# Last weights copied to bf16 beside the convolution passes, router in single steps, and three smaller moves, in a fused convolution, attention and router kernel on eight cores

## The reference

```
xn = layernorm(x)
y  = conv1d(xn, conv_w, 3 taps, 'SAME') + conv_b       # 4096 -> 3 x 1024
q, k, v = split(y, 3)                                  # blocks of 128 tokens
qh, kh, vh = q@wq + bq, k@wk + bk, v@wv + bv           # 16 heads of 64
p  = softmax(causal(qh kh^T / 8))                      # inside each block
s  = (p vh) @ wo + bo;  s = s @ proj_w + proj_b        # 1024 -> 1024 -> 4096
r  = softmax(xn @ router_w^T + router_b)               # 64 experts
w  = r where it is among the 8 largest of its token, else 0
g  = silu(xn * sum(w) + w @ expert_bias)
out = x + s * g
```

## Time and profile before

| | us |
|---|---|
| median of 3 runs (range) | 1099.91 (1096.72 to 1100.67) |
| the profiled execution, its time | 1098.76 |
| its span, slowest core (core 1) | 1097.2 |
| spans of all cores | 1080.7 to 1097.2 |
| PE busy | 1014.8 (92%) |
| DVE busy | 719.1 (66%) |
| ACT busy | 448.0 (41%) |
| POOL busy | 164.6 (15%) |

### The profile page before, as it was taken

How to read it: one execution, slowest core, us unless ns; L and a number is a source line. 1 busy time by engine, 2 the same in 40 slices (tenths; PEclk the granted TensorE clock), 3 DMA queues, 4 the chain that set the end, 5 groups by cost and what they waited for, 6 DMA issues and landing times.

```text
span 1097.2 us, 16289 instructions; the slowest of 8 cores (1080.7 to 1097.2 us)
## 1 busy us (share of the span) xinstructions
PE 1014.8 (92%) x5196; PEld 467.1 (43%) x5196; DVE 719.1 (66%) x1102; ACT 448.0 (41%) x700; POOL 164.6 (15%) x191
## 2 busy tenths in 40 slices
PE   1468998999999999999999999999999999879997
PEld 1235543444444444444444444444444444323332
DVE  6898769666666256666666367777777554355565
ACT  4748533333333243333333255555555213534322
POOL 0134310000000000000000000001110133045555
PEclk9999999999999999999999999999999999989999
DMA  8942327667676587666666566767787798999883
GB/s 260 344 147 87 100 103 231 220 218 228 229 230 215 169 280 263 230 231 230 230 226 214 173 209 218 226 241 231 251 276 216 245 322 264 292 306 309 270 272 144
DMA packets 59072, 251.02 MB, mean 229 GB/s; under 512 B 7494, under 2 KB 7782, under 8 KB 56678
## 3 DMA queue, kind: packets, MB, share of 16 engines
q1 hardware_dynamic: 55372, 241.29, 67.5%
q0 software_dynamic: 2560, 8.57, 2.5%
q10 hardware_dynamic: 1056, 0.11, 0.1%
HBM read 227.05 MB, written 23.09 MB: 228 GB/s over the span
## 4 chain that ended last, share of the span: by engine, by line
PE 71%; DMA 13%; DVE 8%; issue 3%; ACT 2%; SPq 1%; POOL 1%; DVEq 0%; ACTq 0%; POOLq 0%
PE PS L218 69%; DVE AL L225 6%; DMA AL<-cw 4%; DMA AL<-x 4%; DMA AL<-pw 3%; ACT AL L229 2%; PE PS L222 2%; DMA AL<-wo 2%; DVE AL L265 1%; SPq L72 1%; DMA AL<-wv 0%; DMA AL<-eb 0%; ACT PS L231 0%; POOL AL L790 0%; DVEq L58 0%
## 5 line engine op out<-in xcount | busy, mean ns | idle before, releaser
L218 PE MATMUL PS<-AL 128*128 128x512 bf16 (+2 forms) x4608 | 948.0, 373 | 14.4 <-DVE AL L225 13.8
L218 PEld LDWEIGHTS PS<-AL 128*128 128x128 bf16 (+2 forms) x4608 | 418.0, 101 | 528.4 <-issue 62.7
L225 DVE TENSOR_TENSOR AL<-AL 128x512 bf16<-128x512 f32 (+1 forms) x578 | 386.3, 696 | 173.3 <-PE PS L218 118.6
L229 ACT ACTIVATE AL<-AL 128x1024 bf16<-128x1024 f32 (+1 forms) x221 | 232.7, 1055 | 374.7 <-PE PS L218 305.5
L225 DVE TENSOR_TENSOR AL<-PS,AL 128x512 bf16<-128x512 f32 (+2 forms) x145 | 115.5, 797 | 33.3 <-ACT AL L229 18.1
L225 POOL TENSOR_TENSOR AL<-AL 128x512 bf16<-128x512 f32 (+1 forms) x63 | 106.4, 1689 | 182.2 <-DVE AL L225 101.6
L222 PE MATMUL PS<-tI128f,AL 128*128 128x128 f32 (+2 forms) x300 | 44.9, 286 | 52.6 <-ACT AL L229 30.2
L960 DVE SCALAR_TENSOR_TENSOR AL<-AL,tSc,PS 128x1024 f32<-128x1024 f32 x32 | 41.0, 1280 | 65.0 <-PE PS L218 52.1
L229 ACT ACTIVATE AL<-PS 128x512 f32<-128x512 f32 (+2 forms) x88 | 56.8, 669 | 64.5 <-PE PS L222 36.7
L229 ACT ACTIVATE AL<-AL,tScb 128x1024 f32<-128x1024 f32 x32 | 36.8, 1151 | 86.1 <-DVE AL L960 86.1
L72 POOL DMA_DIRECT2D AL<-qhs x16 | 12.1, 756 | 346.6 <-PE PS L218 331.3
(11 more groups left out here) (52 smaller groups left out, 213.9 us busy)
## 6 DMA issues: line engine op xcount, KB each, us to landing
AL<-cw SPq DMA_DIRECT2D x192, 768.0 KB, 5.2
AL<-x SPq DMA_DIRECT2D x16, 1024.0 KB, 30.3
AL<-pw SPq DMA_DIRECT2D x32, 512.0 KB, 6.0
AL<-x SPq DMA_DIRECT2D x32, 512.0 KB, 9.4
out<-AL SPq DMA_DIRECT2D x31, 512.0 KB, 6.9
AL<-wq SPq DMA_DIRECT2D x8, 512.0 KB, 3.8
AL<-wk SPq DMA_DIRECT2D x8, 512.0 KB, 3.9
pts<-AL POOLq DMA_DIRECT2D x16, 256.0 KB, 5.9
```

Source lines behind the costliest of these rows:

```text
L218: return PE.do(lambda e: e.matmul(out, lhsT, rhs, start=start, stop=stop, skip_group_check=skip), *toks, tok=tok)
L225: return eng.do(lambda e: e.tensor_tensor(out, a, b, op), *toks, tok=tok)
L229: return AC.do(lambda e: e.activation(out, in_, func, bias=bias, scale=scale), *toks, tok=tok)
```

## The change

1. **Copies.** 24 new stream entries "copy", two in each of 12 passes (`COPY_P`; behind units 3 and 6). An entry loads one f32 block of `wo` (8), of the first (8) or of the second block of `proj_w` (8) into a staging slot, GpSimd casts it into one of two bf16 buffers that attention uses later (`pbf`, `pts`), and GpSimd's queue stores it to a new DRAM buffer `wbs`. The first attention block waits for the last two stores.
2. **End of the passes.** `wo` and blocks 0 and 1 are loaded from `wbs` in bf16, without staging or cast. Block 2 is staged and cast on GpSimd, block 3 staged and cast on ACT, both ahead of the output stage; `load3` and `cast3` are gone.
3. **x pieces** of the output stage are loaded on GpSimd's queue.
4. **Router.** The eight subtractions of the maximum become one operation with a broadcast operand; the eight masked steps one comparison into a mask `stm`; the eight scalings two products. `drip` gives an entry at units 1 to 4 of a pass only.
5. **v3** is formed by GpSimd while statistics are left (steps 0 to 10), and the even bank is then free when ACT has copied it.
6. **Slots** of attention blocks 7, 8 and 10 to 15 come one slot earlier.

```diff
+        COPY_P = (2, 4, 5, 6, 7, 9, 10, 11, 12, 13, 14, 15)
...
+                if p in COPY_P and g in (3, 6):
+                    stream.append(("copy", 0, 2 * COPY_P.index(p) + g // 6))
...
+            elif kind == "copy":
+                rows = slice(128 * (g % 8), 128 * (g % 8) + 128)
+                src = d_wo[rows, :] if g < 8 else d_pw[rows, 1024 * (g // 8 - 1):1024 * (g // 8)]
+                k = SY.dma(S(f"sF{f}"), fq[f], src, *f_free[f])
+                k = GP.do(lambda e: e.tensor_copy((pbf, pts)[g % 2], fq[f]), k, k_copy[g % 2], tok=True)
+                f_free[f] = [k]
+                k_copy[g % 2] = GP.dma(S(f"sWC{g % 2}"), d_wb[g], (pbf, pts)[g % 2], k)
...
-                k_v3 = tt(DV, vout(3), cc2(bE), E1, ALU.subtract, k_ec, k_p)
+                if n_stat < 32:
+                    tt(GP, vout(3), E0, E1, ALU.subtract, k_ec, k_p, tok=False)
+                    ring[rn % 3] = [k_ec]
+                else:
+                    ring[rn % 3] = [tt(DV, vout(3), cc2(bE), E1, ALU.subtract, k_ec, k_p)]
...
         def r_sub():
-            rd["k"] = each(lambda e, j: e.tensor_scalar(lgt3[:, j, :], lgt3[:, j, :],
-                                                        nm8[:, j:j + 1], None, ALU.add), 8, rd["k"])
+            rd["k"] = tt(DV, lgt3, lgt3, bc(nm8), ALU.add, rd["k"])
...
-            rd["k"] = each(lambda e, j: e.scalar_tensor_tensor(
-                lgt3[:, j, :], lgt3[:, j, :], t8a[:, 8 * j + 7:8 * j + 8], lgt3[:, j, :],
-                ALU.is_ge, ALU.mult), 8)
+            rd["m"] = tt(DV, stm, lgt3, bc(t8a3[:, :, 7]), ALU.is_ge)
 
         def r_norm():
-            rd["k"] = each(lambda e, j: e.tensor_scalar(lgt3[:, j, :], lgt3[:, j, :],
-                                                        rs8[:, j:j + 1], None, ALU.mult), 8, rd["k"])
+            k = tt(DV, lgt3, lgt3, bc(rs8), ALU.mult, rd["m"])
+            rd["k"] = tt(DV, lgt3, lgt3, stm, ALU.mult, k)
...
-        s_at = [1 + 33 * n // 10 for n in range(NHB)]
+        s_at = [1, 4, 7, 10, 14, 17, 20, 23, 26, 30, 33, 36, 39, 42, 46, 49]
...
-                dripped(1)
+                if 1 <= g <= 4:
+                    dripped(1)
...
         for kc in range(8):
-            k_wo = staged(GP, wob[kc], d_wo[128 * kc:128 * kc + 128, :], k_unit23[1])
+            k_wo = SY.dma(S("sWO"), wob[kc], d_wb[kc], *k_copy, k_unit23[1])
+        for i in range(2):
+            for kc in range(8):
+                k_pwl[i] = SY.dma(S(f"sPW{i}"), pwb[i][kc], d_wb[8 * (i + 1) + kc], k_unit23[7])
...
-            k_pwl[1] = stage_pw(AC, 1, kc, k_unit23[7])
+            k_pwl[2] = stage_pw(GP, 2, kc, k_unit23[7])
         for kc in range(8):
-            k_pwl[2] = stage_pw(AC, 2, kc)
+            k_pwl[3] = stage_pw(AC, 3, kc, k_vpe)
...
-                x_tok[m] = SY.dma(S(f"sXG{m % NX}"), xg[m % NX],
+                x_tok[m] = GP.dma(S(f"sXG{m % NX}"), xg[m % NX],
                                   two(d_x[t][:, 1024 * i:1024 * i + 1024]), w)
```

More of the change, by code:

```diff
@@ L111, in build_program @@
     d_pt = dint("pts", [16, 128, 1024])
+    d_wb = dint("wbs", [24, 128, 1024])
     d_pbs = nc.dram_tensor("pbs", [2, 32, 128], BF16, kind="Internal").ap()
@@ L173, in build_program @@
         t8a = f32v(B_KH + 6144, 64)
+        stm = f32v(B_KH + 8192, 512).rearrange("p (j f) -> p j f", j=8)
         nm8 = f32v(B_KH + 6400, 8)
@@ L340, in build_program @@
                 slot += 1
+                if p in COPY_P and g in (3, 6):
+                    stream.append(("copy", 0, 2 * COPY_P.index(p) + g // 6))
         for kind, _, _ in stream:
             ui.append(nu % NU)
-            nu += kind != "w"
+            nu += kind not in ("w", "copy")
         f_free = [[k_ed] for _ in range(NF)]
@@ L347, in build_program @@
         u_ready = [None] * len(stream)
+        k_copy = [None, None]
         def prep(n):
@@ L474, in build_program @@
                     osb[e][:, :, 0:1], edge[:, a:a + 2, s:s + 1]), tok=True)
-                k_v3 = tt(DV, vout(3), cc2(bE), E1, ALU.subtract, k_ec, k_p)
+                if n_stat < 32:
[3 more added lines that the diff above has]
+                    ring[rn % 3] = [tt(DV, vout(3), cc2(bE), E1, ALU.subtract, k_ec, k_p)]
                 k_v0 = tt(GP, vout(0), O0, O1, ALU.subtract, k_ec, k_oc, k_p)
-                tt(DV, vout(1), E0, cc2(bO), ALU.add, k_oc, tok=False)
+                tt(DV, vout(1), E0, cc2(bO), ALU.add, k_ec, k_oc, tok=False)
                 k_v2 = tt(DV, vout(2), cc2(bO), E0, ALU.subtract)
-                ring[rn % 3] = [k_v3]
                 ring[(rn + 1) % 3] = [k_v2]
@@ L553, in router_pe1, with bc @@
             return rd["k"]
+        def bc(z):
+            return z.unsqueeze(2).to_broadcast([128, 8, 64])
         def r_max():
@@ L699, in at_nrm @@
             k = DV.do(lambda e: e.reciprocal(t_rr[:, o:o + 8], t_rs[:, o:o + 8]), a[n]["exp"], tok=True)
-            if n >= 1:
-                DV.wait(a[n - 1]["t"])
+            DV.wait(a[n - 1]["t"] if n >= 1 else k_copy[0])
             a[n]["nrm"] = tt(DV, pbf.rearrange("p (q t) -> p q t", q=8),
@@ L714, in at_pts @@
         def at_pts(n):
-            if n >= 1:
-                AC.wait(a[n - 1]["sp"])
+            AC.wait(a[n - 1]["sp"] if n >= 1 else k_copy[1])
             a[n]["pts"] = act(pts, bT, AF.Copy, a[n]["t"])
@@ L763, in build_program @@
                     evac(p)
-            elif kind != "w":
+            elif kind in ("q", "k"):
                 if g == 0:
@@ L795, in stage_pw @@
             return staged(eng, pwb[i][kc], d_pw[128 * kc:128 * kc + 128, 1024 * i:1024 * i + 1024], *toks)
-        for kc in range(8):
-            k_wo = staged(GP, wob[kc], d_wo[128 * kc:128 * kc + 128, :], k_unit23[1])
-        k_z = DV.do(lambda e: e.memset(pbhl, 0.0), k_unit23[7], tok=True)
         k_pwl = [None] * 4
         for kc in range(8):
-            k_pwl[0] = stage_pw(GP, 0, kc, k_unit23[7])
+            k_wo = SY.dma(S("sWO"), wob[kc], d_wb[kc], *k_copy, k_unit23[1])
+        k_z = DV.do(lambda e: e.memset(pbhl, 0.0), k_unit23[7], tok=True)
+        for i in range(2):
+            for kc in range(8):
+                k_pwl[i] = SY.dma(S(f"sPW{i}"), pwb[i][kc], d_wb[8 * (i + 1) + kc], k_unit23[7])
         for i in range(2):
@@ L924, in build_program @@
         w_last = []
-        k_st3 = [None] * 8
-        def load3(k):
-            if k < 8:
-                k_st3[k] = SY.dma(S(f"sST{k % 4}"), stg[k % 4],
-                                  d_pw[128 * k:128 * k + 128, 3072:4096], *st_free[k % 4])
-        def cast3(k):
-            k_pwl[3] = act(pwb[3][k], stg[k % 4], AF.Copy, k_st3[k], k_vpe)
-            st_free[k % 4] = [k_pwl[3]]
         for m in range(NX):
             load(m)
-            if m < 4:
-                load3(m)
         PE.wait(last["o"], a[7]["o"], *vfree[0], *vfree[1], k_eb, k_pb)
@@ L965, in build_program @@
                 finish(m - 1)
-            if m in range(2, 18, 2):
-                cast3(m // 2 - 1)
-                load3(m // 2 + 3)
         finish(NM - 1)
```

## The result

The changed kernel takes 1118.8 us (median; 1116.0 to 1120.6, and one execution of 1168.0) against 1099.9 us for the kernel before: a ratio of 1.0175, 95% interval 1.0144 to 1.0206. In the execution of 1168.0 the cores of one die had a granted clock of 0.92 to 0.95 where the others had 0.99; executions of that kind are left out of all medians, ranges and ratios here. The kernel is slower by 19 us where 14 us less were forecast. The profiled execution took 1119.94 us. Here, as there, the slowest core counts, and now all eight are late.

The account below looks back on a forecast made before the run. TensorE's work plus a few holes was taken as the bound, with DVE the bound from 40 to 84 us. Terms -6.5 - 4.3 + 1.5 - 4.4 = -13.7 gave 1085.1, median 1086 us; range 1077 to 1096.

Parts of the forecast that it names:

- Copies, "I take +1.5 us": Copies beside the 12 passes: mostly hidden, costing 1.5 us in all.
- rival 3: Copies starve the passes: slots turn in 9.06 us, passes 30.2 us, total 1116, starting above 6.8 us latency; chance 0.06 in full.
- mean 7.3: hidden: Copy passes: conv loads hold slots 7.6 us, copies about 6; mean 7.3 fits the 8.3 us available per turn.
- the latency at 5.5 us: Copy passes: assumed conv load latency, giving 7.6 us in a slot with about 2.1 us of transform.
- the cast at 1.04 us: Copy passes: each copy's GpSimd cast takes 1.04 us, on an engine said to be idle there.
- the rule for two SBUF inputs: GpSimd and a two-SBUF-input DVE operation exclude each other for a whole instruction; early differences were judged to lose nothing.
- The share of 0.88: Passes with two copies: DMA share rises from 0.67 to about 0.88.
- Early differences, -6.5 us: Transposing stage, steps 0 to 10: DVE, the bound, gives GpSimd one of three differences, saving 11 x 0.593 = 6.5 us.
- rival 4: Transposing stage: GpSimd or ACT paces the early steps, shrinking the 6.5 us gain to 1 or 2; total 1091, chance 0.06.
- Router, -4.3 us: Start of pass 2: the 3.05 us hole shrinks, gaining 2.65 us, plus 1.7 us of clock; together 4.3 us.
- Slots, taken as 0 with bounds ±2: Attention: moved slots shift which evacuations have an exp block ahead; holes of 0.3 to 1.6 us merely change place.
- End, -4.4 us: Before output piece 2: the first Silu waits behind ACT's fourth-block casts instead of late x; TensorE resumes 4.4 us earlier.

Follow-up runs that it names:

- no_copies: Changed kernel with last weights and output stage as before, keeping early differences, router and slots: 1089.7 us, ratio 0.9893.
- own_place: Changed kernel with copy loads in a buffer of their own, each still taking an unused turn in the staging rotation: 1119.5 us, ratio 1.0185.
- own_slot: Changed kernel with copy loads in a buffer of their own, taking no place in the staging rotation: 1090.8 us, ratio 0.990.
- router_only: Kernel before with only the router's steps of the change: 1100.1 us, ratio 1.0009.

## Why the prediction was wrong

- **Copies, "I take +1.5 us": the step that failed.** The passes lost 28 us against before and 30 against no_copies, which is rival 3 in full where 1.5 were forecast: 12 passes of 30.1 us (27.6 + 30.0/12) where that rival has 30.2. Rival 3 says 1116 us in all, and 1118.8 were measured. Three things in the step were wrong.
  - It averaged the turns ("mean 7.3: hidden"), as if a copy that is done in 6 us gave its spare time to the unit loads. It cannot: loads are issued in order, and the slot passed over is the next unit's loss; own_place gives a copy no time in a slot at all and is as slow, where the average would be 0.8 x (6.0 + 2.1) = 6.5 us a turn of the 8.3 at hand. (With 6.8 us of latency the step has 8.5 for the mean turn and rival 3 has 8.3; the terms give 8.3.)
  - It took the latency at 5.5 us as something given, when the places themselves bunch the loads, to 9.01 us in the chain above.
  - It took the cast at 1.04 us and at no cost to DVE, though it had the rule for two SBUF inputs in hand and tried it on the early differences: the transforms' sums have two such inputs, and in the changed kernel the casts lengthened 18 of them per core. How the 30 us divide between late loads and lengthened sums is open.
- **Rival 3 had it.** With a turn of 3/10 of 30.1, that is 9.0 us, a latency of 5.9 and 2.1 of transform leave 1 us of waiting for the list ahead; the 9.06 us between issues in the earlier trace rows already held all of it. The row that measured the turn directly was in hand and was given a chance of 0.06, because the sum from parts came out lower. That it hits the pass to 0.1 us is in part luck, since it was taken beside other traffic: two empty places give 28.1 us a pass, a turn of 8.4. That its start was put at 6.8 us of latency was wrong too: own_slot runs at 6.6 without a loss, and the changed kernel starves at 5.9.
- **The share of 0.88 was reachable.** own_slot has 0.91 with no hole, so "GpSimd is idle there" and the DMA engines' room were rightly judged. The order of the slots was not, nor what the casts do to DVE's sums.
- **Early differences, -6.5 us: right.** End of pass 0 is at 149.7 us on the mean core against 155.2, so 5.5 us; rival 4 is out. No run has these differences alone; nothing else of the change stands ahead of that point.
- **Router, -4.3 us: mis-sized.** It was read on core 1, where pass 2 went from 32.5 to 27.6 us, as forecast (4.9). But the mean core won 1.5 us in the passes (2.8 in pass 2, less 1.3 in pass 8), and the time of the slowest core did not move: in router_only the slowest is core 3, which lost its time in the last passes and at a last hole of 7.95 us. A hole that some cores have and others do not is no gain of the maximum while later stages scatter by as much.
- **Slots, taken as 0 with bounds ±2: 3.2 us,** outside them. With it the parts other than copies and end give 11 us, near the 10.8 of the sum, which is chance. The 3.2 us are from one profiled execution of each kernel; the ratio fell from 1.0009 to 0.9958, some 5.6 us, with intervals that just fail to meet.
- **End, -4.4 us: mechanism right, worth nothing in the time.** The chain goes through loads of pw, the last cast, the table load and the Silu, as said, and the hole was 5.91 us, with 3.8 forecast. But own_slot, with that end, is no quicker than no_copies with the old one (1090.8 and 1089.7), where the old hole spreads over 2.3 to 14.5 us on the cores and the new one over 1.3 to 9.7. The 4.4 us were read on the slowest core, and the mean hole went only from 5.5 to 5.1 us. That the fourth block should leave the way, worth 9 to 11 us, was not seen.
- **What stays open.** Beside the share of the casts, the last 3 us between rival 3's 1116 and the measurement have no account of their own; the clock's 4.9 us are part of the 30. A fourth slot in the rotation was not tried, nor wv's loads, one entry in three behind the last units, in a buffer of their own: no_copies still has waits of 1.1 to 1.3 us there on core 3.

## What to carry to other kernels

An entry in a rotation of staging slots costs its place, not its duration: with loads issued in order, count entries per slot in the stretch and multiply by a turn measured beside the same traffic, and do not average quick entries with slow ones. The place is free while that product stays under the stretch's own time (one empty entry a pass: 9 x 9.06 / 3 = 27.2 us, under 27.6). Give side traffic a buffer outside the main rotation, even where the DMA engines have room. Where a row of the trace shows the same pattern whole, as the 9.06 us between issues did, trust it over a sum from parts; and take the gain of a hole from all cores, not from the slowest.

## What the runs showed of the hardware

- Unit loads of 768 KB landed after 4.8 us (median, core 0) evenly spaced and 5.9 us bunched, with the same bytes; with copies beside them and evenly issued, 6.6 us at a DMA share of 0.91, and no hole.
- GpSimd's cast of 128x1024 and a DVE sum with two SBUF inputs take turns. On core 0 of the changed kernel a cast alone takes 1.04 us. One that starts while such a sum is running mostly ends 0.90 us behind that sum's end, in two cases 1.50 us behind it, up to 1.6 us long in all, and a sum that starts within a cast takes 1.27 to 1.56 us instead of 0.69 in 18 of 19 cases. The casts of wv do the same in the kernel before (1.50 us at 857.5, core 1), while the 16 staged ones, without such sums beside them, take 1040 ns. The Trainium skill (SBUF — State Buffer, "Who interferes with whom") says that a DVE operation with two SBUF inputs and a GpSimd one that reads SBUF contend, and that the other waits for the whole instruction. The trace agrees, to within the 0.14 us by which the waiting cast is shorter. In own_slot this cost no time. Where the place makes the slots tight it is in the chain, as the pair of rows at 257.90 shows. The row of the casts, of the groups of GpSimd after:

```profile
L380 POOL CAST AL<-AL 128x1024 bf16<-128x1024 f32 x24 | 30.2, 1257 | 361.3 <-DMA AL<-pw 201.4 <-DMA AL<-wo 159.9
```
